# Half of batch 0's MLP moved from the first interval into the last batch's interval, with the first interval and its loads reordered

## Time and profile before

| | us |
|---|---|
| median of 3 runs | 2260.81 (2257.69 to 2263.62) |
| the profiled execution | 2264.27 |
| its span, first to last instruction | 2260.7 |
| PE busy | 2158.7 (95%) |
| DVE busy | 1436.7 (64%) |
| ACT busy | 1434.9 (63%) |
| POOL busy | 1091.0 (48%) |
| mean granted TensorE clock | 0.986 of 2.4 GHz |

### The profile page before, as it was taken

One profiled execution on the slowest core, in us unless ns is written; L12 is line 12 of the kernel. 1 busy time (PEld: TensorE's weight loads), 2 busy tenths in 40 slices (PEclk: granted clock), 3 DMA queues, 4 the chain that ended last, 5 costly groups with the idle time before them and its releaser, 6 DMA issues.

```text
span 2260.7 us, 48434 instructions
## 1 busy us (share of the span) xinstructions
PE 2158.7 (95%) x16260; PEld 1402.0 (62%) x16260; DVE 1436.7 (64%) x2108; ACT 1434.9 (63%) x1669; POOL 1091.0 (48%) x1065
## 2 busy tenths in 40 slices
PE   3799999999999999999999999999999999999985
PEld 2656666666666666666666666656666666666632
DVE  5656676676757666675766767667576766666521
ACT  2166675757667576666757666675766657666672
POOL 3544545454545545354554545546455454544420
PEclk9899999999999999999999999999999999999997
DMA  3334462634535364553635445363454635445342
GB/s 120 110 107 131 99 193 84 184 106 123 180 92 183 91 172 115 131 175 83 189 99 146 138 115 182 84 196 104 130 158 97 192 87 168 119 126 157 96 129 59
DMA packets 167656, 296.79 MB, mean 131 GB/s; under 512 B 25008, under 2 KB 112816, under 8 KB 155056
## 3 DMA queue, kind: packets, MB, share of 16 engines
q1 hardware_dynamic: 167472, 294.01, 45.6%
HBM read 173.32 MB, written 102.76 MB: 122 GB/s over the span
## 4 chain that ended last, share of the span: by engine, by line
PE 82%; DVE 6%; ACT 4%; issue 4%; POOL 2%; DMA 1%; SPq 0%; DVEq 0%; ACTq 0%; POOLq 0%
PE pair L986 31%; PE pair L1173 20%; PE pair L1156 15%; PE pair L1137 15%; ACT probs L643 3%; DVE count L862 2%; PE pair L998 1%; DVE stats L725 1%; POOL rot L538 1%; PE pair L1070 1%; DMA qk_dram<-rot_b 1%; ACT h_sq L634 1%; POOL probs L556 1%; DVE h_sq L846 1%; DVE denom L785 1%
## 5 line engine op out<-in xcount | busy, mean ns | idle before, releaser
L643 ACT ACTIVATE probs<-pair 128x1024 f32<-128x1024 f32 x1152 | 1116.4, 1026 | 490.7 <-PE pair L1156 490.3
L556 POOL TENSOR_SCALAR_AFFINE_SELECT probs<-probs 128x512 f32<-128x512 f32 x512 | 376.7, 756 | 507.4 <-ACT probs L643 507.4
L548 POOL TENSOR_TENSOR h_lo<-h_sq,h_hi 128x512 fp32r<-128x512 f32 x256 | 385.8, 1507 | 427.6 <-DVE h_hi L848 427.1
L1173 PE MATMUL pair<-probs,v_sb 128*17 128x512 f32 (+3 forms) x6144 | 551.4, 492 | 4.4 <-DVE numer L882 3.4
L1156 PE MATMUL pair<-q_ring,k_ring 64*128 64x512 f32 (+3 forms) x3072 | 443.1, 382 | 22.2 <-ACT probs L643 20.8
L846 DVE TENSOR_TENSOR h_sq<-h_sq 128x512 f32<-128x512 f32 x256 | 202.8, 792 | 330.9 <-ACT h_sq L634 330.8
L1156 PEld LDWEIGHTS pair<-q_ring,k_ring 64*128 64x128 f32 x3072 | 227.3, 185 | 282.8 <-ACT probs L643 183.9
L1173 PEld LDWEIGHTS pair<-probs,v_sb 128*17 128x17 f32 x6144 | 152.6, 97 | 298.9 <-issue 263.9
L862 DVE SCALAR_TENSOR_TENSOR count<-y_sb,count 128x512 bf16<-128x512 f32 x256 | 296.8, 1159 | 6.7
L1137 PE MATMUL pair<-wproj_hi,h_hi 128*128 128x256 f32 x1024 | 292.8, 286 | 4.3 <-POOL h_lo L548 4.3
L1137 PE MATMUL pair<-wproj_lo,h_hi 128*128 128x256 f32 x1024 | 289.6, 283 | 0.0
(11 more groups left out here) (87 smaller groups left out, 2572.2 us busy)
## 6 DMA issues: line engine op xcount, KB each, us to landing
q_ring<-qk_dram SPq DMA_DIRECT2D x384, 128.0 KB
k_ring<-qk_dram SPq DMA_DIRECT2D x384, 128.0 KB
qk_dram<-planes SPq DMA_DIRECT2D x64, 512.0 KB, 2.8
qk_dram<-rot_b SPq DMA_DIRECT2D x64, 512.0 KB, 4.0
xn<-in_x SPq DMA_DIRECT2D x16, 1024.0 KB, 7.0
rs<-in_x SPq DMA_DIRECT2D x64, 256.0 KB, 2.8
acc_dram<-rs SPq DMA_DIRECT2D x64, 256.0 KB, 4.5
attn<-numer SPq DMA_DIRECT2D x256, 64.0 KB, 2.3
```

Of the source, the lines that this page charges most:

```text
L548: pool.tensor_tensor(h_lo[i % HB][:, :], h_sq[i % HB][:, :], h_hi[i % HB][:, :].bitcast(F32), ALU.subtract).then_inc(h_lo_done, 1)
L556: ins = pool.affine_select(view, view, [[0, 4], [1, P]], ALU.is_ge, 0.0, base=0, channel_multiplier=-1)
L643: act.activation(probs[BUFFER[n]][:, 2 * pr:2 * pr + 2, :], pair[m % NSLOT][:, :, :], ACT.Exp, scale=SCALE).then_inc(exp_done, 1)
L1173: ins = pe.matmul(pv_bank[32 * i:32 * i + VW, q0 - g * G:G], v_sb[:, kt, 4 * quad + i, :], probs[BUFFER[n]][:, i, at:at + width(kt, g)], s ...
```

## The change

- `MLP_FIRST` and `MLP_FINAL`: interval -1 computes only items 0 to 7 of batch 0's MLP. Items 8 to 15 are computed in interval 15. For that, interval 14 loads batch 0's x again and normalises it as the other intervals do for theirs (`x_at=0`), and interval 15 transposes it (16 transposes) and splits it. Its expands stand at steps 3 to 8, 10 and 12, its contracts at steps 7 to 9 and 11 to 15.
- Batch 0's output is stored without that half's counts. In interval 15 SP loads rows 512 to 1023 of `out` back into rs at step 13 (`load_back`), DVE counts at steps 16 and 17, and SP stores them again at step 17 (`store_back`), ahead of the last gather. Interval 0 has no counts for steps 8 to 11 (`bare`): two semaphore increments stand in.
- Output projections of interval 15 use two other banks in turn (`final_bank`), and their waits change with them.
- The start: SP loads wfc and wproj before wv. DVE clears q_ring and the value bank before its statistics, POOL clears k_ring, and issues one `pow` on constants before it waits for the variance. ACT makes wqk's and wfc's high parts at once, wproj's at step 4 and wv's at step 9. POOL makes the low parts of wfc (directly behind `root(0)`) and of wproj (at step 6), DVE that of wv (at step 12).
- Interval -1: `norms` and `bound` move from step 7 to step 8 (in another bank), the bias product to step 12, and all of batch 1's normalisation to step 13. PE waits at its end for the bias, the shift and wv's low part.

The fallback program is adapted to the new counts of the semaphores. The core of the diff:

```diff
-EXPAND_AT = {6: 0, 7: 1, 8: 2, 9: 4, 11: 7, 12: 8, 13: 10, 14: 11, 15: 13, 16: 14}
-EXPAND_LATE = {8: 3, 10: 6, 12: 9, 14: 12, 16: 15}
-EXPAND_EARLY, CONTRACT_EARLY = {10: 5}, {10: 3}
-CONTRACT_AT = {8: (0,), 9: (1, 2), 10: (4,), 11: (5, 6), 12: (7,), 13: (8, 9), 14: (10,), 15: (11, 12), 16: (13,),
-               17: (14, 15)}
+MLP = ({10: 5}, {10: 3}, {6: 0, 7: 1, 8: 2, 9: 4, 11: 7, 12: 8, 13: 10, 14: 11, 15: 13, 16: 14},
+       {8: (0,), 9: (1, 2), 10: (4,), 11: (5, 6), 12: (7,), 13: (8, 9), 14: (10,), 15: (11, 12), 16: (13,), 17: (14, 15)},
+       {8: 3, 10: 6, 12: 9, 14: 12, 16: 15})
+MLP_FIRST = tuple({n: x for n, x in t.items() if (max(x) if isinstance(x, tuple) else x) < NFT} for t in MLP)
+MLP_FINAL = ({}, {}, {3: 8, 4: 9, 5: 10, 6: 11, 10: 14, 12: 15},
+             {7: (8,), 8: (9,), 9: (10,), 11: (11,), 12: (12,), 13: (13,), 14: (14,), 15: (15,)}, {7: 12, 8: 13})
...
-Y0_AT, Y1_AT = 12, 17
+Y0_AT, Y1_AT, Y_FINAL_AT = 12, 17, 15
 SPIKES_HERE = {8 + 2 * a + part: (a, part) for a in range(2) for part in range(2)}
+SPIKES_FINAL = {16 + a: a for a in range(2)}
...
-XN_AT = {16: range(0, 4), 17: range(4, 8)}
+XN_AT, XN_FIRST = {16: range(0, 4), 17: range(4, 8)}, {13: range(NT)}
...
-            for n, (dst, src) in enumerate(((wqk_in, wqk), (wv_in, wv), (wfc_in, wfc), (wproj_in, wproj))):
+            for n, dst, src in ((0, wqk_in, wqk), (2, wfc_in, wfc), (3, wproj_in, wproj), (1, wv_in, wv)):
                 sp.dma_start(dst[:, :, :], src.rearrange("(k p) n -> p k n", p=P)).then_inc(w_in[n], 16)
-                if n == 0:
+                if n == 2:
...
+            def load_back():
                 for a in range(2):
+                    alone(sp, acc_out[a], B * 2 * 16)
+                    alone(sp, out_sent[2 + a], 16)
+                    sp.dma_start(rs[a][:, :, :], rows(out, 0)[:, 4 + 2 * a:6 + 2 * a, :]).then_inc(rs_in[a], 16)
+            def store_back():
+                for a in range(2):
+                    alone(sp, acc_done, B * 4 + a + 1)
+                    sp.dma_start(rows(out, 0)[:, 4 + 2 * a:6 + 2 * a, :], rs[a][:, :, :]).then_inc(acc_out[a], 16)
...
+                    if final and n == 13:
+                        load_back()
...
+                    if final and n == 17:
+                        store_back()
...
+            interval(B - 2, True, True, True, True, x_at=0)
+            interval(B - 1, True, True, False, False, final=True)
+            last_output(B - 1, B - 1, False)
+            for a in range(2):
+                alone(sp, acc_out[a], (B * 2 + 1) * 16)
...
+            pool.memset(neg_half[:, :], -0.5).then_inc(warm, 1)
+            pool.memset(ln_b[:, :], 1.0).then_inc(warm, 1)
             pool.memset(v_sb[:, :, :, DK:VW], 1.0).then_inc(cleared, 1)
-            pool.memset(neg_half[:, :], -0.5).then_inc(ln_step, 1)
-            pool.memset(q_ring[:, :, :, :].bitcast(F32), 0.0).then_inc(cleared, 1)
-            pool.wait_ge(ln_step, 1)
+            pool.memset(k_ring[:, :, :, :].bitcast(F32), 1.0).then_inc(cleared, 1)
+            pool.wait_ge(warm, 2)
+            pool.tensor_tensor(ln_a[:, :], ln_b[:, :], neg_half[:, :], ALU.pow).then_inc(warm, 1)
+            pool.wait_ge(warm, 3)
...
+            def low_weight(n):
+                hi, lo, whole = ((wfc_hi, wfc_lo, wfc_in), (wproj_hi, wproj_lo, wproj_in))[n - 2]
+                pool.wait_ge(w_hi[n], 1)
+                pool.tensor_tensor(lo[:, :, :], whole[:, :, :], hi[:, :, :].bitcast(F32), ALU.subtract).then_inc(w_lo[n], 1)
...
+                    if first and n == 6:
+                        low_weight(3)
...
             root(0)
-            pool.memset(k_ring[:, :, :, :].bitcast(F32), 1.0).then_inc(cleared, 1)
-            interval(-1, False, False, True, True, True)
+            low_weight(2)
...
-                    if first and n == 3:
-                        for w in range(1, 4):
-                            high_weight(w)
...
+                    if first and n == 4:
+                        high_weight(3)
...
+                    if first and n == 9:
+                        high_weight(1)
             high_weight(0)
-            interval(-1, False, False, True, True, True)
-            act.wait_ge(w_lo, 4)
+            high_weight(2)
+            interval(-1, False, False, True, True, first=True)
...
+                        if not bare:
+                            spikes(halves_before(b, again) - 1, added, a, range(3 * part, 3 * part + 3), biased)
+                        elif part:
+                            alone(dve, rs_biased, biased)
+                            dve.sem_inc(acc_done, 1)
...
+                    if final and n in SPIKES_FINAL:
+                        a = SPIKES_FINAL[n]
+                        spikes(half_of(b, 1, first, final, again), B * 4 + a, a, range(STEPS + 1))
...
-                    if first and n == 4:
-                        for w in range(1, 4):
-                            low_weight(w)
...
+                    if first and n == NORM_AT + 1:
+                        bound(nb, first_norm_bank)
                         replicate_bias()
...
+                    if more and not first and n == Y1_AT or final and n == Y_FINAL_AT:
+                        take_y(half_of(b, 1, first, final, again), item + NFC - 1)
+                    if first and n == 12:
                         whole_bias()
+                        low_weight(1)
...
+            dve.memset(q_ring[:, :, :, :].bitcast(F32), 0.0).then_inc(cleared, 1)
+            dve.memset(pv_bank, 0.0).then_inc(cleared, 1)
...
+            interval(0, True, False, True, True, bare=True)
...
+                if final and i == NFT:
+                    pe.wait_ge(xT_lo_done, nb * 4 + 4)
+                elif i:
+                    pe.wait_ge(relu_done, item + i)
...
+                    if final and f == 0:
+                        pe.wait_ge(out_done, (b - 1) * 4 + half + 3)
+                    elif i == 0:
+                        if half and first:
+                            pe.wait_ge(rot_done, nb * 4 + 4)
...
+                    if more and n == NORM_AT and not first:
+                        norms(nb, norm_bank)
+                    if (more or final) and n in expand_at:
+                        if first and expand_at[n] == 0:
+                            pe.wait_ge(w_lo[2], 1)
+                        expand(b, nb, item, expand_at[n], last, final)
+                    if first and n == NORM_AT + 1:
+                        norms(nb, first_norm_bank)
+                    for i in contract_at.get(n, ()) if more or final else ():
+                        if first and i == 0:
+                            pe.wait_ge(w_lo[3], 1)
+                        contract(b, nb, item, i, last, first, final)
+                    if (more or final) and n in expand_late:
+                        expand(b, nb, item, expand_late[n], last, final)
+                    if first and n == 12:
                         pe.wait_ge(wo_in, 16)
                         pe.wait_ge(bias_rep, KD)
                         split_product(bias_bank, [(bv_rep[:, k, :], wo_sb[:, k, :]) for k in range(KD)]
...
+            pe.wait_ge(shift_used, 1)
+            pe.wait_ge(w_lo[1], 1)
...
+            interval(B - 1, True, True, False, False, final=True)
```

More of the change, by code:

```diff
@@ L557, in mask, with interval @@
                 ins.then_inc(mask_done, 1)
-            def interval(b, att, last, more, norm, first=False):
+            def interval(b, att, last, more, norm, first=False, final=False, again=False):
                 nb = b + 1
+                item = first_item(b, first, final, again)
+                expand_early, contract_early, expand_at, contract_at, expand_late = mlp_of(first, final)
                 for n in range(NSTEP):
@@ L623, in take_v, with rectify @@
                     "p (t h d) -> p t h d", t=2, d=DK), ACT.Copy).then_inc(v_copied, 1)
[L625 removed]
+            def rectify(nb, item, i):
                 if i < 2:
@@ L648, in high_weight, with interval @@
                 act.wait_ge(w_in[n], 16)
-                act.activation(hi[:, :, :], whole[:, :, :], ACT.Copy).then_inc(w_hi, 1)
-            def interval(b, att, last, more, norm, first=False):
+                act.activation(hi[:, :, :], whole[:, :, :], ACT.Copy).then_inc(w_hi[n], 1)
+            def interval(b, att, last, more, norm, first=False, final=False, again=False):
                 nb = b + 1
+                tb = nb + again
+                item = first_item(b, first, final, again)
+                expand_early, contract_early, expand_at, contract_at, expand_late = mlp_of(first, final)
                 for n in range(NSTEP):
@@ L657, in interval @@
                         take_v(b, m)
-                    if more and n in EXPAND_EARLY:
-                        rectify(nb, EXPAND_EARLY[n])
+                    if (more or final) and n in expand_early:
+                        rectify(nb, item, expand_early[n])
                     if att:
@@ L763, in rotate @@
```

(35 more changed lines are left out.)

309 lines of the change are left out of this document (157 added, 152 removed).

## The result

| | before | changed |
|---|---|---|
| median of 6 runs each, us | 2262.58 (2257.69 to 2270.97) | 2247.03 (2241.19 to 2250.4) |
| ratio, 95% interval | | 0.9924 (0.99 to 0.9949) |
| profiled execution, us | 2264.27 | 2244.92 |
| its span, us | 2260.7 | 2243.2 |
| its mean granted clock | 0.986 | 0.987 |

A forecast was written before the change was run, and what follows sets the result against it. The prediction took PE, busy 95% of the span, as the bound over the long middle. Head -35.2, interval 0 +2 and interval 15 +6.5 gave -26.7, from 2260.8 to 2234 us, range 2225 to 2249.

The forecast's parts named there:

- Intervals 1 to 14: The full intervals after interval 0: unchanged, with 14 loading and normalising like the others; 0, at most +0.5 us.
- The start: Up to batch 0's first transposes: first pow paid behind the memsets, root ending 3.9 us earlier, transposes 2.5 us earlier.
- The normalisation beside the w_fc half: In the start: POOL's w_fc low part, 4.8 us, holds up the first normalisation; net +1.3 us, bounds -3.1 and +2.2.
- Interval -1: Batch 0 alone, before interval 0: item 7 ends at 86.7, interval 0 starts at 90.0 against 125.18, -35.2 us.
- The step through unit 3: In interval -1: unit 3's `low_qk` ends at 61.3 against 69.0, 7.7 us earlier, 2.5 of them the start.
- Interval 0, +2: Normalisation, bias additions and counts follow wv's low part, so PE waits for the first split; +2 us, bounds 0 and +6.
- Interval 15, +6.5: Last interval: PE's work 100.5, open holes and one slow run sum to 108.2 against 101.7 us; bounds -1 and +24.9.
- Rival A: The head gives less, by POOL's subtractions blocking more or interval 0 waiting 6: 9 us less, 2243; chance 0.15.
- B: Interval 15 fills nothing, each added piece having its own wait: +24.9 in place of 6.5, 2252 us; chance 0.13.
- C: The head gives more: normalisation not blocked, shorter first code load, PE's clock up; another 8 us, 2226; chance 0.10.
- D: Slower: counts and `store_back` ahead of the last gather, interval 15 and tail gain 42 against 33 saved; 2270; chance 0.02.

The follow-up runs named there:

- x12: x11 with ACT's loop covering intervals 1 to 14 instead of 1 to 13; 2241.24 us against x11's 2239.46.
- x1: The changed kernel once more, unedited; 2252.89 us.
- x2: The changed kernel with 64 semaphore increments added at the head of ACT's stream; 2241.67 us, ratio 0.9901.
- x4: The changed kernel with SP's loads behind w_fc held until POOL's constant pow is done; 2245.31 us.
- x6: The changed kernel with all of SP's loads held until POOL's constant pow is done; 2255.99 us.
- x3: The changed kernel with POOL waiting for all eight normalisations before it makes w_fc's low part; 2236.52 us.
- x9: The kernel before with the changed start alone, biases and all of the MLP staying where they were; 2264.03 us, ratio 0.9997.
- x10: x9 with six useless matmuls in each of steps 8 to 17 of interval 15; 2253.83 us, ratio 0.9934.
- x11: The changed kernel with the edits of x3, x4 and x8, and w_proj's halves earlier; 2239.46 us, ratio 0.9878.
- x7: The changed kernel with items 8 to 15, their counts and two transfers left out of interval 15, transposes kept; 2236.93 us.
- x8: The changed kernel with expand 14 moved between the two scores of step 10 in interval 15; 2243.03 us.
- x13: x11 with 64 semaphore increments ahead of ACT's first instruction, as in x2; 2234.92 us, ratio 0.9851.

## Why the prediction was right or wrong

The direction was right, and 2247.03 lies near the upper end of 2225 to 2249. The forecast gain of 26.7 was 9.2 us too large in the spans; two steps carry it.

- **"Intervals 1 to 14. Unchanged ... 0, at most +0.5"** is the step that failed: +9.0 in interval 14, none in 1 to 13. I costed its work, which is in fact hidden (x12: 133.46). Not counted was that a changed program puts ACT's instructions elsewhere, so that ACT's pause falls on an exponential that PE waits for (x1, x2, x12): 6.5 us of waiting and 2.5 of a fallen clock. That the pause is an instruction fetch, long because it stands behind the ring loads, fits all eleven pauses but was not tested by itself.
- **The start, "4.54 + 7.67".** The term was mis-sized: 10.97 in place of 7.67, because the weight loads now move from the start of that wait on (x4, x6: 9.41 and 7.45 with part and all of them held). The root ended at 20.63, 0.6 earlier than before, where 3.9 was forecast. The normalisation beside the w_fc half cost what was forecast (the first four 5.55 us in the chain against 4.54, +1.0; forecast +1.3); x3 shows that it need not be paid at all. Together 2.9 us lost.
- **Interval -1.** The step through unit 3 was right: `low_qk` ended at 64.2, 4.8 earlier than before, which is the 7.7 forecast less those 2.9. Item 0's contract came at 69.56, another 0.5 lost, and item 7's ended at 91.7 instead of 86.7, since it now waits 1.31 us for its h_lo, which item 8's expand used to cover; I had taken that expand's 1.4 as pure gain. From item 7's end to the first scores it took 2.6 (bias product, its sum, wv's low part), not 3.3. Together 2.9 + 0.5 + 1.6 - 0.7 = 4.3. x9 splits the gain of 30.9: 2.9 for the new start, 28.0 for the items that moved.
- **Interval 0, +2.** It was -0.5. The step failed by a size: the counts took 9.6 us (98.73 to 108.32) where 11.7 was taken, so DVE was free 14.0 us into the interval, not 17, before the split that PE needs.
- **Interval 15, +6.5.** Measured +5.8, its clock 0.98, a tail of 29.6. The sum (PE's work plus the open holes plus one slow run) came out, in part by terms that cancel: PE stood open for 4.4 us, not 6.3, and was busy for 103.2, not 101.9. And the reading of it hid something: the moved half costs 10.8 us over a filled interval (107.5 against x10's 96.7), and 5.0 come back because the interval before ran partly at half clock. With both numbers the sum is the same 5.8.
- **Rival A** (the head gives less) describes the head as it came, 4.3 us of the 9 it named; it missed where the rest went. **B** fell: PE waits 4.0 us for the exponentials and nowhere for h_lo or masks. **C** fell in the changed kernel, but x11, which takes the normalisation out from behind POOL and holds part of the loads, reaches 87, beyond the 90 of the forecast. **D** fell: the tail is shorter than before.

## What to carry to other kernels

An idle stretch of TensorE can cost twice, once for the wait and again for the matmuls after it at half the clock, so work put into its gaps may be nearly free, and taking work out may gain nothing (x7: 23 us out, 0.7 gained). When a profile of a changed program shows an engine standing still with no releaser, look at the instruction queues and at the transfers issued just before it, and shift the code or the transfer ahead of redesigning the work. The price of an operation's first use should be measured beside the transfers that it will meet: here holding the later loads for it won 1.9 us of the head (x4), and holding all of them lost 5.8 (x6).

## What the hardware did that was not expected

- ACT paused 2.2 to 8.2 us once in its first run of code behind a loop, at the same instruction in all eight profiles with the same number of ACT instructions up to there (the changed kernel, x1, x3, x4, x6, x7, x8, x11), and at another after 64 more instructions or with a longer loop. DVE did the like in interval 14 of x9 and x10, for 4.29 and 3.48 us at a count, where nothing waited for it (133.2 us).
- The first pow on POOL cost 7.45 us with no transfer beside it, 9.4 to 9.9 with the loads up to w_fc (x4, x11, x12, x13), and 11.0 to 12.4 with all of them issued first.
- TensorE's granted clock in one and the same interval was 0.87 (x9), 0.93 (before) and 1.00 (with junk matmuls in the gaps); between the first and the last lie 11 us of its length.
